# Expert rows that carry their own destination, and block outputs scattered to token order by GpSimd

## What is computed

```python
x = layernorm(x + attention(x))      # 16 query heads, 4 key heads of 8, causal, rope, tanh-capped scores
x = layernorm(x + cross_block(x))    # cross attention to 32 context rows, FiLM, S4D convolution, feed-forward
x = layernorm(x + moe(x))            # below
# moe: 8 experts, 2 chosen per token, and 2 shared experts that every token passes
shared = mean over 2 of (gelu(x @ sW1 + sb1) @ sW2 + sb2)
w      = softmax over the two largest of (x @ rW + rb)
moe    = shared + sum over the two chosen e of w_e * (gelu(x @ W1_e + b1_e) @ W2_e + b2_e)
```

## Time and profile before

| what | value |
|---|---|
| median of three executions | 547.97 us |
| the profiled execution | 549.56 us |
| its span | 547.7 us |
| granted TensorE clock, mean | 0.875 |
| PE busy | 412.9 us (75%) |
| DVE busy | 371.3 us (68%) |
| ACT busy | 333.4 us (61%) |
| POOL busy | 262.3 us (48%) |

### The profile page before, as it was taken

The page is one execution under the profiler, slowest core; times in us unless marked ns, Lnnn a source line. Parts: engine busy times, 40 slices in busy tenths (PEclk is TensorE's granted clock), DMA queues, the critical chain, the costliest instruction groups (busy, mean ns, idle before and its releaser), DMA issues.

```text
span 547.7 us, 9136 instructions
## 1 busy us (share of the span) xinstructions
PE 412.9 (75%) x2857; PEld 265.2 (48%) x2857; DVE 371.3 (68%) x1080; ACT 333.4 (61%) x585; POOL 262.3 (48%) x306
## 2 busy tenths in 40 slices
PE   3664545765889878879879989988999997799800
PEld 2251132433534343434334476457587886788700
DVE  1987798587966878698894899996187524622144
ACT  2669869999798696877968426214466453355300
POOL 2407977676542167271856174625045507500272
PEclk9976567867778997899779999999999999999955
DMA  3797000000059500000001000184559787899212
GB/s 99 178 384 304 0 1 5 7 1 5 3 137 199 114 1 1 1 2 0 2 1 38 1 2 0 39 242 130 184 161 293 228 268 239 251 293 283 76 49 57
DMA packets 45893, 58.56 MB, mean 107 GB/s; under 512 B 9627, under 2 KB 34966, under 8 KB 45846
## 3 DMA queue, kind: packets, MB, share of 16 engines
q1 hardware_dynamic: 37174, 50.78, 31.2%
q0 software_dynamic: 2048, 4.20, 2.5%
q10 hardware_dynamic: 6624, 3.02, 1.9%
HBM read 42.23 MB, written 20.46 MB: 114 GB/s over the span
## 4 chain that ended last, share of the span: by engine, by line
DVE 33%; PE 25%; issue 11%; POOL 10%; ACT 9%; DMA 6%; SPq 3%; POOLq 0%; ACTq 0%; DVEq 0%
POOL y_pair L1191 5%; ACT probs L978 4%; DMA x_blk<-expert_rows 4%; PE bank_o L703 4%; PE ring_g L862 3%; PE ring_g L781 3%; PE ring_s L854 3%; ACT probs L984 2%; PE ring_g L583 2%; DVE stats L1395 2%; PE ring_s L689 2%; PE ring_g L786 2%; SPq L477 2%; DVE xn L1406 2%; DVE hn L1406 1%
## 5 line engine op out<-in xcount | busy, mean ns | idle before, releaser
L978 ACT ACTIVATE probs<-ring_s 128x512 f32<-128x512 f32 (+1 forms) x192 | 88.2, 541 | 34.7 <-PE ring_s L689 34.5
L1027 ACT ACTIVATE g_ring<-ring_s,w_blk 128x128 f32<-128x128 f32 x184 | 52.2, 370 | 55.8 <-PE ring_s L854 43.2
L1137 POOL TENSOR_SCALAR_AFFINE_SELECT probs<-probs 128x256 f32<-128x256 f32 (+1 forms) x96 | 54.4, 600 | 63.8 <-ACT probs L984 63.6
L984 ACT ACTIVATE probs<-probs 128x2560 f32<-128x2560 f32 x32 | 75.1, 2348 | 0.8
L689 PE MATMUL ring_s<-qT,kT 64*128 64x128 bf16 (+3 forms) x256 | 53.3, 340 | 27.9 <-ACT probs L978 24.6
L1191 POOL DMA_INDIRECT y_pair<-expert_out,y_rows x32 | 31.0, 969 | 63.7 <-issue 45.3
L1079 POOL TENSOR_TENSOR rstd<-var_eps,neg_half 128x4 f32<-128x4 f32 x24 | 25.0, 1045 | 62.2 <-DVE var_eps L1400 53.4
L703 PE MATMUL bank_o<-probs,vv 128*32 128x128 f32 (+3 forms) x512 | 46.9, 516 | 7.9 <-POOL probs L1137 7.9
L854 PE MATMUL ring_s<-xT_blk,w_blk 128*128 128x128 f32 x368 | 48.4, 277 | 5.2 <-DVE xT_blk L1706 5.2
L1020 ACT ACTIVATE g_ring<-ring_s,vcols 128x512 f32<-128x512 f32 x32 | 21.8, 688 | 49.3 <-PE ring_s L827 19.4
L854 PEld LDWEIGHTS ring_s<-xT_blk,w_blk 128*128 128x128 f32 x368 | 44.7, 192 | 10.1 <-issue 9.9
(11 more groups left out here) (339 smaller groups left out, 902.3 us busy)
## 6 DMA issues: line engine op xcount, KB each, us to landing
w_blk<-expert_pack SPq DMA_DIRECT2D x46, 578.0 KB, 5.0
expert_rows<-zero_rows SPq DMA_DIRECT2D x2, 4096.0 KB, 20.0
expert_pack<-in_L_ffn_W SPq DMA_DIRECT2D x16, 256.0 KB
x_blk<-expert_rows SPq DMA_DIRECT2D x46, 64.0 KB, 4.1
expert_out<-y_blk ACTq DMA_DIRECT2D x46, 64.0 KB, 4.3
x<-in_x SPq DMA_DIRECT2D x4, 256.0 KB, 3.2
w_sh<-in_L_ffn_sW SPq DMA_DIRECT2D x4, 256.0 KB, 4.8
out<-x SPq DMA_DIRECT2D x4, 256.0 KB, 3.0
```

The costliest lines, as they stand in the source:

```text
L978: f(probs[:, pair % NPROB, BASE[n]:BASE[n] + WIDTH[n]], s_bank("sc", b, p, n)[:, 0:WIDTH[n]], ACT.Tanh, scale=1.0 / (CAP * float(np.sqrt(n ...
L984: f(probs[:, pair % NPROB, :], probs[:, pair % NPROB, :], ACT.Exp, scale=CAP).then_inc(exp_done, 1)
L1027: last = f(g_ring[:, u % RING, P * n:P * (n + 1)], s_bank("bu", k)[:, P * n:P * (n + 1)], ACT.Gelu, bias=w_blk[:, k % SLOTS, HID + n:HID + ...
L1137: last = g.affine_select(out=v, in_=v, compare_op=ALU.is_ge, fill=0.0, base=0, pattern=[[0, v.shape[1]], [1, P]], channel_multiplier=-1)
```

## The change

A row of `expert_rows` gets a 129th number: where in token order this row's output belongs. x2 is kept with 129 columns per tile; `numbers`, a new first step of VectorE, makes the tokens' numbers from `before_bf` and `index`. A token's second expert's row must carry another number (the token's plus 2048), so ScalarE copies x2 to `x2_again` (`again:b`) and VectorE writes the other number beside it in `rows_of`. `x2_again` is one buffer: copy and number of batch b wait for the scatters of batch b−1. The table is filled by one DMA of rows of 129 (zeros, and a number that marks an empty row).

VectorE's `bx:k` takes each row's number out of `x_blk` into `spot`, where an empty row's becomes one past the end. The block store moves from ScalarE's queue to GpSimd, as one indirect DMA per block that scatters 128 outputs to token order. So `y_places` goes, and `fetch` becomes two plain DMAs of 256 KB per batch on SP: group 0's behind `load_block(30)`, group 1's behind the last block. `final(b, n)` works on all four tiles in four passes (first expert, second, statistics, aggregates) and not tile by tile. `load_block` also waits for `spot_ready` of the block whose slot it takes; `x_blk` moves to the part of SBUF that attention uses before. Loads of both layers in one row per partition are as they were.

All four lists are new. Beside the lines shown, attention and cross-block steps are permuted by a few places; ScalarE's fold steps of the start stand behind `states`, `place:0` and `select:0` a little later among the film steps, ScalarE's list has no stores, and TensorE's has `bt:23` ahead of `bd:21`. `bias` follows `steps`.

```diff
-ZERO_ROWS = 8
+
+XW = D + 1
+NOWHERE = 2 * B * SEQ
+NONE = float(1 << 20)
...
+SPOTS = 2 * SLOTS
...
-rms:0 vectors rroot:0 bias steps vv:0 ctabs parts:0 states copies:0 states2 states3 pack rms:1 rroot:1 args:0.0
+numbers rms:0 vectors rroot:0 steps bias vv:0 ctabs parts:0 states copies:0 states2 states3 pack rms:1 rroot:1
...
+by:23 by:24 bx:27 by:25 bx:28 by:26 bx:29 by:27 bx:30 fin:0.0 fin:0.1 fin:0.2 fin:0.3 by:28 by:29 fo:0 by:30 bx:31
+fin:1.0 fin:1.1 fin:1.2 fin:1.3 bx:32 bx:33 fo:1 by:31 by:32 by:33 bx:34 bx:35 bx:36 by:34 by:35 bx:37 bx:38 bx:39
...
-root:2.1 root:1.2 mask:27 h:1 xn:2 mask:28 mask:29 scatter:0 mask:30 mask:31 root:3.1 shape:2 ffn:1 root:2.2 root:0.3
-root:4.1 root:1.3 h:2 xn:3 scatter:1 root:3.2 ffn:2 root:4.2 shape:3 root:2.3 h:3 root:3.3 ffn:3 root:4.3 scatter:2
-scatter:3 fetch:0.0 fetch:0.1 fetch:0.2 fetch:0.3 fetch:1.0 fetch:1.1 root:5.0 fetch:1.2 fetch:1.3 root:5.1 fetch:2.0
-fetch:2.1 fetch:2.2 fetch:2.3 fetch:3.0 fetch:3.1 root:5.2 fetch:3.2 fetch:3.3 root:5.3
+root:2.1 root:1.2 h:1 xn:2 mask:27 mask:28 mask:29 scatter:0 mask:30 mask:31 root:3.1 shape:2 ffn:1 root:2.2 root:0.3
+root:4.1 root:1.3 h:2 xn:3 scatter:1 root:3.2 ffn:2 root:4.2 shape:3 store:0 root:2.3 store:1 h:3 store:2 store:3
+store:4 store:5 root:3.3 store:6 ffn:3 store:7 root:4.3 scatter:2 store:8 store:9 store:10 store:11 store:12 scatter:3
+store:13 store:14 store:15 store:16 store:17 store:18 store:19 store:20 store:21 store:22 store:23 store:24 store:25
+store:26 store:27 root:5.0 store:28 store:29 store:30 root:5.1 store:31 store:32 store:33 store:34 store:35 store:36
+store:37 store:38 store:39 store:40 store:41 store:42 store:43 store:44 store:45 root:5.2 root:5.3
...
-            zero_rows = tb("zero_rows", [P, ZERO_ROWS * D])
-
-        x2 = sb("x2", [P, B, NT * D])
+            zero_rows = tb("zero_rows", [P, XW])
+
+        x2 = sb("x2", [P, B, NT, XW])
+        x2_again = sb("x2_again", [P, NT, XW])
...
-        x_blk = sb("x_blk", [P, SLOTS, D])
...
+            x_blk = eb("x_blk", [P, SLOTS, XW])
...
-        rows_dram = nc.dram_tensor("expert_rows", (sum(GROUP_ROWS), D), F32, kind="Internal").ap()
-        y_dram = [nc.dram_tensor(f"expert_out{g}", (NB[g] * P, D), F32, kind="Internal").ap() for g in range(GROUPS)]
+        rows_dram = nc.dram_tensor("expert_rows", (sum(GROUP_ROWS), XW), F32, kind="Internal").ap()
+        y_dram = nc.dram_tensor("expert_out", (NOWHERE + SPOTS * P, D), F32, kind="Internal").ap()
...
-            for g in range(GROUPS):
-                at, n = ROW0[g], NE * CAPACITY[g]
-                load(rows_dram[at:at + n, :].rearrange("(p n r) w -> p n (r w)", p=P, r=ZERO_ROWS),
-                     zero_rows[:, :].unsqueeze(1).broadcast_to([P, n // (P * ZERO_ROWS), ZERO_ROWS * D]), blanked)
-                load(rows_dram[at + n:at + GROUP_ROWS[g], :].rearrange("(p r) w -> p (r w)", p=P), zero_rows[:, 0:(NE - 1) * D], blanked)
+            blank = rows_dram.rearrange("(n p) w -> p n w", p=P)
+            load(blank, zero_rows[:, :].unsqueeze(1).broadcast_to([P, sum(GROUP_ROWS) // P, XW]), blanked)
...
+                    sp.wait_ge(spot_ready, k - SLOTS + 1)
...
+            def fetch(g):
+                for n in range(SLOTS):
+                    sp.wait_ge(y_sent[n], 16 * len(range(n, BLOCK0[g] + NB[g], SLOTS)))
+                for b in range(FROM[g], FROM[g] + SIZE[g]):
+                    if b >= 2:
+                        sp.wait_ge(pair_used, b - 1)
+                    for k in range(2):
+                        at = (k * B + b) * SEQ
+                        load(y_pair[:, b % 2, :, k, :], y_dram[at:at + SEQ, :].rearrange("(j p) d -> p j d", p=P), pair_landed[b % 2])
 
             sp.wait_ge(pv_done, B * NQUAD)
             sp.wait_ge(ld_pack, 16 * (3 * NE + 2))
@@ -570,6 +583,9 @@
                 sp.wait_ge(scattered[g], 16 * 2 * NT * SIZE[g])
                 for q in range(NB[g]):
                     load_block(BLOCK0[g] + q)
+                    if g and q == SLOTS + 1:
+                        fetch(g - 1)
+            fetch(GROUPS - 1)
...
-            def store_block(k):
-
-                g, q = BLOCKS[k]
-                act.wait_ge(*g_freed("bd", k))
-                act.dma_start(y_dram[g][P * q:P * (q + 1), :], y_blk[:, k % SLOTS, :]).then_inc(y_sent[k % SLOTS], 16)
-
-            play(ACT_ORDER, {"store": store_block, "masks": masks, "fold1": fold1, "fold2": fold2, "fold3": fold3, "fold4": fold4,
+            def x2_copy(b):
+                act.wait_ge(x2_ready, b + 1)
+                if b:
+                    act.wait_ge(scattered[GROUP[b - 1]], 16 * 2 * NT * (b - FROM[GROUP[b - 1]]))
+                f(x2_again[:, :, 0:D], x2[:, b, :, 0:D], ACT.Copy).then_inc(x2_copied, 1)
...
-                op(g.memset(zero_rows[:, :], 0.0))
-                g.memset(kbd[:, :], 0.0)
+                op(g.memset(zero_rows[:, 0:D], 0.0))
+                then()
+                g.memset(zero_rows[:, D:XW], NONE).then_inc(blank_ready, 1)
+                g.memset(kbd[:, :], 0.0).then_inc(kbd_ready, 1)
                 g.memset(neg_half[:, :], -0.5)
...
+                g.affine_select(out=before_bf[:, :], in_=ones_bf[:, :], compare_op=ALU.is_gt, fill=0.0, base=0,
+                                pattern=[[1, P]], channel_multiplier=-1).then_inc(before_ready, 1)
...
-                    pool.wait_ge(blanked, 16 * 2 * GROUPS)
+                    pool.wait_ge(blanked, 16)
                 pool.wait_ge(rows_ready, b + 1)
-                for j in range(NT):
-                    for k in range(2):
+                for k, x in enumerate((x2[:, b, :, :], x2_again[:, :, :])):
+                    if k:
+                        pool.wait_ge(x2_copied, b + 1)
+                    for j in range(NT):
                         g.indirect_dma_start(out=rows_dram, out_offset=bass.IndirectOffsetOnAxis(ap=rows_i[:, k, b * NT + j:b * NT + j + 1], axis=0),
-                                             in_=x2[:, b, D * j:D * (j + 1)], in_offset=None).then_inc(scattered[GROUP[b]], 16)
-
-            def fetch(b, j):
...
+                                             in_=x[:, j, :], in_offset=None).then_inc(scattered[GROUP[b]], 16)
+
+            def store_block(k):
+
+                slot = k % SLOTS
+                pool.wait_ge(spot_ready, k + 1)
+                pool.wait_ge(*g_freed("bd", k))
+                to = bass.IndirectOffsetOnAxis(ap=spot[:, k % SPOTS:k % SPOTS + 1], axis=0)
+                g.indirect_dma_start(out=y_dram, out_offset=to, in_=y_blk[:, k % SLOTS, :], in_offset=None).then_inc(y_sent[k % SLOTS], 16)
...
+            def numbers():
+                dve.wait_ge(before_ready, 1)
+                one(v.tensor_reduce(token[:, 0:1], before_bf[:, :], AX, ALU.add))
+                one(ts(moved[:, :], token[:, 0:1], -1.0, float(P - 1), ALU.mult, ALU.add))
+                dve.wait_ge(ld_s4, 16 * 7)
+                one(stt(out=token[:, :], in0=index[:, 0:B * NT], scalar=float(P), in1=moved[:, 0:1].broadcast_to([P, B * NT]), op0=ALU.mult, op1=ALU.add))
+                one(ts(nowhere[:, :], token[:, 0:SPOTS], float(NOWHERE), None, ALU.add))
...
+                ts(x2[:, b, :, D:XW], token[:, b * NT:(b + 1) * NT].unsqueeze(2), 0.0, None, ALU.add)
...
-            def y_places(g):
...
+                if b:
+                    dve.wait_ge(scattered[GROUP[b - 1]], 16 * 2 * NT * (b - FROM[GROUP[b - 1]]))
+                op(ts(x2_again[:, :, D:XW], token[:, at].unsqueeze(2), float(B * SEQ), None, ALU.add))
...
+                slot, n = k % SLOTS, k % SPOTS
+                if k >= SPOTS:
+                    dve.wait_ge(y_sent[slot], 16 * (k // SLOTS - 1))
+                dve.wait_ge(xs_landed[slot], 16 * (k // SLOTS + 1))
+                tt(spot[:, n:n + 1], x_blk[:, slot, D:XW], nowhere[:, n:n + 1], ALU.min).then_inc(spot_ready, 1)
...
-            def final(b, j):
...
+            def final(b, n):
+                tiles = range(NT)
+                if n < 2:
+                    if n == 0:
+                        dve.wait_ge(settled, b + 1)
+                        dve.wait_ge(pair_landed[b % 2], 16 * 2 * (b // 2 + 1))
+                        if b:
+                            dve.wait_ge(y_out_ready, b)
+                    for j in tiles:
+                        at = b * NT + j
+                        op(stt(out=acc[:, b, j, :], in0=y_pair[:, b % 2, j, n, :], scalar=w_sel[:, n, at:at + 1],
+                               in1=acc[:, b, j, :], op0=ALU.mult, op1=ALU.add))
+                    then()
+                elif n == 2:
+                    for j in tiles:
+                        op(v.bn_stats(stats[:, j, :], acc[:, b, j, :]))
+                    then()
                 else:
+                    for j in tiles:
+                        last = v.bn_aggr(mean_var[:, OUT, j, :], stats[:, j, :])
+                        if j < NT - 1:
+                            op(last)
                     last.then_inc(pair_used, 1)
...
```

(27 more changed lines are left out.)

177 lines of the change are left out of this document (70 added, 107 removed).

## The result

The changed kernel took 552.56 us, median of 6 runs (549.69 to 553.83), against 547.81 (545.53 to 548.53) of the kernel before beside it: ratio 1.0068, 95% interval 1.0036 to 1.0099. On a second chip it took 549.41 (12 runs) against 549.03: 1.0014, 0.9987 to 1.0040. So it is slower by 4 to 5 us on the first chip and not measurably on the second. The prediction gave 545.5 and "faster" as the likeliest; the time lies inside its range, the direction is wrong. The profiled execution took 551.91 us with a span of 549.5.

A forecast was written before the change was run, and what follows sets the result against it. Bound: a long chain of waits between four engines running hand-written lists. 6.0 − 1.0 + 0.6 + 3.8 − 1.0 + 0.5 − 3.5 − 7.8 = −2.4 gave 547.2 us profiled, 545.5 median; range 538 to 553.

The forecast's parts named there:

- Start: Head of VectorE's list: `numbers` waits for seven small loads, so `rms:0` starts at 17.0 instead of 11.04 us; +6.0.
- swallowed: Rival: the start's 6 us delay is taken up by later waits that don't shift; 539.5 us, chance 0.22.
- Reordered lists: Attention lists: the same steps in another order cost nothing; 0, with 3 us either way.
- Bookkeeping: VectorE's film and spectra stage of batch 3: dropping `y_places` outweighs the added small operations; −1.0 (0 to −1.8).
- copies of x2: ScalarE copies x2 four times at 0.60 us, once inside attention; +0.6 (0 to 2.4).
- −1.0 and +0.5 for the moved stores: Block stores: ScalarE's GELUs no longer stand behind store waits, −1.0; stores 0 to 7 precede steps in GpSimd's list, +0.5.
- Queue before group 1: GpSimd's list: `store:8` to `store:12` stand before `scatter:3`, which starts 3.8 us late; +3.8 (0 to 5).
- Finals of batches 0 and 1: Expert blocks: without VectorE's waits for gathered rows, TensorE's stall at 457 to 477 us mostly goes; −3.5 (0 to −5).
- End: After the last evacuation: plain fetches replace sixteen gathers, so batch 3 ends at 535.5 instead of 543.34; −7.8 (−5 to −10).
- Blanking: Filling the table by rows of 516 bytes ends between 52 and 81 us, before the first kernel store at 85; 0.
- Late landing: Rival: scatters under load land after 6 us, not 2.2, delaying VectorE in `rows_of(3)`; 551.5 us, chance 0.27.
- rule on GpSimd's shared interfaces: GpSimd stores issued beside VectorE would stretch by contention; five at 1.30 us would add 1.7 us to the sum.

The follow-up runs named there:

- a5: Steps of the kernel before put in the changed kernel's lists (no `numbers`, GpSimd's fetches kept): 557.3 us, ratio 1.0168 to the kernel before.
- a3: Changed kernel with batch 3's ranking, weights and placing moved ahead and store 12 put behind `scatter:3`: 546.12 us, 0.9945 of the kernel before.
- a1: Changed kernel with only `numbers` moved behind `bias` in VectorE's list: 543.97 us, 0.9901 of the kernel before.
- a2: Changed kernel's steps in the lists of the kernel before, `numbers` behind `bias`, `scatter:3` ahead of `store:12`: 551.81 us, 1.0061 of the kernel before.
- a9: Changed steps in the old lists, with `numbers` behind `pack` and final sums of batches 0 and 1 later, in pieces: 543.85 us, 0.9930 of the kernel before.
- b4: Kernel before, pieces of the final sums of batches 0 and 1 each five block steps later, `root:5.0` moved too: 568.93 us, 1.0049, slower chip.
- c2: Changed kernel with `numbers` and batch 3's ranking moved, final-sum pieces of batches 0 and 1 spread one per block step: 558.89 us, 0.9867, slower chip.
- e1: Changed kernel with `numbers` and batch 3's ranking moved, weighted sums and norm statistics of batches 0 and 1 left out: 557.93 us, 0.9850, slower chip.
- b3: Kernel before with its region blanked row by row, 512 bytes each, instead of in long runs: 565.49 us, 0.9981, on a slower chip.
- c1: Changed kernel with batch 3's ranking moved and `numbers` behind `pack` instead of `bias`: 541.71 us, 0.9868 of the kernel before.
- b2: Kernel before with final sums of batches 0 and 1 moved behind blocks 30 and 34, each batch in one piece: 555.04 us, 1.0114.

## Why the prediction was wrong, by its steps

- **Start, +6.0.** Right in size and mechanism: +6.05 in the trace, 6.2 and 6.8 us in two runs. The rival "swallowed" (0.22) is refuted, though the placings looked like it: +6.9, +2.5, +1.1. What hid the delay there were the new lists, which place batch 2 8.0 us earlier in the kernel with the old steps. Two effects of opposite sign look like slack in a difference of two traces.
- **Reordered lists, "0, with 3 us either way".** The net, 2.9 us won by batch 3's placing, just lies in this range, but it is the difference of two larger effects that I did not look for. With the old steps (a5) the new lists win 8.0 us up to batch 2's placing and lose 5.1 between the placings of batches 2 and 3. That the ranking's place is part of this loss is shown by a3, where moving it with `place:3` and store 12 gives back 3.6 and 1.9 us between these placings.
- **Bookkeeping −1.0, copies of x2 +0.6.** At batch 2's placing a1 stands 2.8 us behind a5, which has nearly the same lists and the old steps; 0.7 of it is there by the first exp (46.23 against 45.51). I had put −0.4. The −1.0 and +0.5 for the moved stores were not tried apart.
- **Queue before group 1, +3.8.** Mechanism right, size more than twice too high: the scatter starts 3.6 us behind the placing and not 1.6, and from placing to block 23's load it takes 18.8 us (18.5 in the other execution) where it took 17.3, +1.2 to +1.5. With the placing so late, stores 8 to 11 were through; only store 12 stood in the way. The whole group started 8.7 us late as my terms' sum of 8.9 has it, but for other reasons: start 6.3, lists 8.0 won and 5.1 lost, 2.8 of small steps, 1.5 of queue and 1.0 more between the placings that I can't name. That agreement was luck, as the other execution with 4.6 shows.
- **Finals of batches 0 and 1, −3.5.** The step that failed, and with its place in the sum the direction. I took TensorE's missing 3.8 us in 457 to 477 for the price of VectorE's wait, and all of it for time that would be won. Without the wait the last group took 74.6 us (76.8 in the other execution) against 74.0, and not 70.5. What I forecast did happen, TensorE waits 3.6 us less for VectorE's copies, but it waits 5.0 us more for the rows of blocks (in the last group alone 3.0 before, 7.9 and 10.6 now), a wait that my sum did not have. With the new steps in the old lists (a2, a9) it is 1.6, so it goes with the new order; what in the order makes it was not tried. That the wait was worth nothing in the kernel before is what b4 says, with the reservation made there; a9 shows that such a wait in one piece can cost. c2 and e1 show no cost of the lumps or the sums in the new lists, to 2 to 4 us. Put at 0, the term leaves 550.7 for a profiled execution, and no gain.
- **End, −7.8.** Right: −8.6, in all kernels with the new steps (20.3 to 20.7 us against 28.9 to 30.5).
- **Blanking, 0.** Right, by b3 for rows of 512 bytes, and by the trace for those of 516, which were done at 83.1 us, ahead of the first kernel store (91.63 in this kernel). In c1 they were done at 87.8, behind that kernel's first store (86.19); what that costs was not tried. The two packets per row behind my upper bound of 81 us were wrong, see below.
- **Late landing (rival, 0.27, 551.5 us).** Its time was near, its place was not: scatters land in 3.0 and 3.5 us at the median and not 6, and VectorE does not wait in `rows_of(3)`. It comes there 9.4 us after the last scatter of batch 2 was issued, though, so that a landing of 6 us would not have shown either.
- **Output.** From the last normalisation's end to the span's end 5.6 us instead of 4.4, in every kernel with x2 in rows of 129. Not foreseen (+1.2), and not tried apart.

From the forecast to the profiled 551.91: 547.2 + 3.5 (finals) + 0.5 (last group) − 0.2 (its start) − 0.8 (end) + 1.2 (output) + 0.5 (around the span) = 551.9. The medians differ by more than the profiled executions because the kernel before was profiled 1.75 above its median of six and the changed one 0.65 below its own. The Trainium skill's rule on GpSimd's shared interfaces (GPSIMD Engine Reference, Specifications) did not decide: of 33 stores from 440 to 526 us 30 took 0.96 us and three 1.03 to 1.12.

## What to carry to other kernels

A step put at the head of an engine's hand-written list cost the whole of its slowest wait here, even if what it makes is needed 280 us later: put it where its result is first due. A wait in a trace is a cost only if something on the chain stands behind it, and removing it pays only if the next wait there is not as long: look which waits TensorE has left. One wait of 8.0 us cost some 5 us in the old lists (a2, a9). Moving a wait away can cost more than it, if it becomes a stretch of work that holds back short steps (b2). When steps and order are changed together, exchange them (old steps in the new order, new in the old) before judging either.
